# Grouped conv by unshifted blocks, its outer part shifted by DMA

## The chip, the cores and the metric

One core of a Trainium2 chip. The metric is the device time in microseconds (us) of one execution; three executions of the kernel before are shown. The profile is of one further execution.

## The reference

The input x has 128 batches of 64 channels and 1024 positions, in float32. Two layers follow each other, each with a residual:

```python
x = x + _L0_ffn_ref(_L0_cond_ref(x, cond_128, ...), ...)
x = x + _L1_ffn_ref(_L1_cond_ref(x, cond_128, ...), ...)
```

- Layer 0, condition: a 64x64 matrix per batch (a softmax mixture of 8) times the channels, plus a bias per channel.
- Layer 0, ffn: a base product 1024x1024 plus a mixture of 8 low-rank experts of rank 16, gated by a softmax over 8 logits minus a threshold.
- Layer 1, condition: a 1D convolution over the 1024 positions with 9 taps, padding 4, in 4 groups of 16 channels, plus a context value per channel.
- Layer 1, ffn: a base product 1024x1024 plus the same kind of low-rank experts, the two largest of 8 logits weighted by a softmax.

```python
out = lax.conv_general_dilated(x, weight, window_strides=(1,), padding=[(4, 4)],
                               dimension_numbers=('NCH', 'OIH', 'NCH'), feature_group_count=4)
```

## The kernel before, in words

A tile is 128 rows (2 batches x 64 channels) of 1024 positions. There are 64 tiles per layer (STEPS = 64), so 128 steps, n = 0 to 127; layer 1 begins at n = 64. Each float32 operand of a product is split into a high part (float32r) and a low part, and a product is hi x hi + hi x lo + lo x hi.

A step n does on TensorE (`step`, L856) the base product of tile n, and woven into it the condition of tile n+1 (`mix`, L762) and the tail of tile n-1 (`turn`, L814, and `up`, L822):

- `base` (L792, matmuls at L807): for k = 0 to 7, three products of Y's 128 columns k against the weights, each over three PSUM banks of about 387 columns, 9 matmuls per k. It accumulates in psB, 3 banks per parity of n. At k = 0 and 4 it waits for the halves of Yhi and Ylo (`yhi_half`, `ylo_half`).
- `mix`: 4 chunks c, each of two blocks k = 2c, 2c+1 of 128 positions, into bank c % 2 of psT. Chunk c follows base tile k = MIX_AFTER[c], that is k = 0, 1, 2, 3. In layer 0 a block has two matmuls with the mixing matrix M (L781, L782). In layer 1 it has four: for each of two windows w of the input, one of 256 columns (Xhi against CT hi and lo, L787) and one of 128 (Xlo against CT hi, L789).
- `turn` (after k = 4, L820) transposes the gated expert values hw; `up` (after k = 5, L833) adds the expert product to psB with 6 matmuls of 512 columns.

In layer 1 the partition of Xraw is (r, i): r one of 8 residues of the position block, i one of 16 channels of a group, and the free axis is (b, q), b one of 8 blocks of 16 channels (2 batches x 4 groups), q one of 128 position blocks of 8 positions. `load_x` (L209) fetches it from x1_scratch by 8 DMAs, one per r (L222), with a shift of 4 residues, so that 9 taps around a block of 8 outputs lie in the windows q and q+1 of one shifted row; that is why Xraw, Xhi and Xlo have 129 columns per b (QP, XW), one of them zero.

VectorE (DVE), `step` at L714: the gates of tile n-1 (`weigh`, L693, from the copy L699 to hw at L705); `evacuate_y` (L546), two adds per chunk from psT to Y (L566, L568); `split_y` (L570), Ylo by halves (L575); `low_ht` (L709); `add_rest` (L585); `emit` (L592), which writes outb of tile n-1 in three adds (L605) and counts `o_done`.

ScalarE (ACT), `step` at L469: exponentials of the gates, Yhi by halves (L431), Xhi of tile n+2 (`high_x`, L407, L417), the copy HThi of the turned values (`high_ht`, L515). At the last step of layer 0 also the split of layer 1's weights (`split_w`, L443).

GpSimd (POOL), `step` at L367: Xlo of tile n+2 (`low_x`, L327, L333) and the residual plus bias of tile n+1 in res (`residual`, L344, L352 and L362).

SyncE (SP), `step` at L256, issues the DMAs, one queue in this order: Xraw and row of tile n+2 (L213 or L222, L224); the store of tile n-1 (`store`, L297, issue L301) behind a wait for `o_done`; in layer 1 res of tile n+1 (L294). Layer 0 stores into x1_scratch, layer 1 into out.

All orders are written out by hand; the engines meet at counting semaphores. Y is one buffer, Yhi, Ylo, res, outb and Xraw have two, Xhi and Xlo one.

Of the kernel before, what the change touches and what calls it, by code (L numbers as in the profile page):

```python
# [27 lines left out]
P = 128  # L28
# [8 lines left out]
TAPS, PAD = 9, 4  # L37
# [12 lines left out]
QP = Q + 1  # L50
XW = BG * QP
MODES = 8
MIX_AFTER = (0, 1, 2, 3)
MIX_AFTER_FIRST = (1, 3, 4, 5)
TURN_AFTER, UP_AFTER = 4, 5
# [13 lines left out]
def build(nc, x, condw, condr, mixw, l0w, l0b, l0B, convw, l1w, l1b, l1B, out):  # L69
    NT = x.shape[0]  # L70
    STEPS = NT // P
    x1 = nc.dram_tensor("x1_scratch", [NT, H], F32).ap()
    rows = nc.dram_tensor("row_scratch", [2, STEPS, P], F32).ap()
    atts = nc.dram_tensor("att_scratch", [2, STEPS, MODES], F32).ap()

    with ExitStack() as ctx:
# [11 lines left out]
        CT = sb("CT", [P, G, 2, 2, P], F32R)  # L88
        bias = sb("bias", [P, H])

        Xraw = sb("Xraw", [P, 2, XW])
        Xhi, Xlo = sb("Xhi", [P, XW], F32R), sb("Xlo", [P, XW], F32R)
# [6 lines left out]
        mixT = sb("mixT", [P, MODES, C])  # L99
        prod = sb("prod", [P, MODES, C])  # L100
# [62 lines left out]
        pad_zero = sem("pad_zero")  # L163
# [10 lines left out]
        def as_f32(ap):  # L174
            return ap.bitcast(F32)

# [31 lines left out]
        def _(sp):  # L208
            def load_x(j, par, layer):  # L209

                n = 2 * j + par
                if layer == 0:
                    sp.dma_start(Xraw[:, par, 0:H], x[bass.ds(n * P, P), :]).then_inc(x_loaded[par], 16)  # L213
                else:

                    dst = Xraw[:, par, :].rearrange("p (b q) -> p b q", b=BG)
                    m = n - STEPS
                    src = x1[bass.ds(m * P, P), :].rearrange("(b i) (r q) -> r i b q", b=BG, r=BR)
                    for r in range(BR):
# [36 lines left out]
            def step(j, par, lay0, lay, lay1, lay2):  # L256
                n = 2 * j + par
                if lay2 is not None:
# [5 lines left out]
                    if lay2 == 1:  # L264
                        if lay == 0:
                            sp.wait_ge(pad_zero, par + 1)
                        sp.wait_ge(stored[par], 16 * (j - STEPS // 2 + 2))
                    load_x(j + 1, par, lay2)
                if lay == 0 and isinstance(j, int) and n == 0:
# [6 lines left out]
                    for r in range(BR):  # L276
                        to = craw[r * GC:(r + 1) * GC, :, :, :].rearrange("p g w (t o) -> p g w t o", o=GC)

                        sp.dma_start(to[:, :, 0, 0:r + 1, :], convw[:, :, BR - r:BR + 1, :]).then_inc(conv_in, 16)
                        sp.dma_start(to[:, :, 1, r:BR, :], convw[:, :, 0:BR - r, :]).then_inc(conv_in, 16)  # L280
# [15 lines left out]

            def store(j, par, layer):  # L297
# [3 lines left out]
                sp.dma_start(to[bass.ds((n - layer * STEPS) * P, P), :], outb[:, par, :]).then_inc(stored[par], 16)  # L301

            run(sp, step)
            store(STEPS - 1, 1, 1)
            for par in range(2):
                sp.wait_ge(stored[par], 16 * STEPS)
# [3 lines left out]
        def _(pool):  # L310
# [8 lines left out]
            pool.memset(stage[:, :, NW - 1:NW], 0.0).then_inc(consts, 1)  # L319

# [6 lines left out]
            def low_x(j, par, layer):  # L327
                n = 2 * j + par
                w = (H if layer == 0 else XW) // PIECES
# [37 lines left out]
            def step(j, par, lay0, lay, lay1, lay2):  # L367
# [7 lines left out]
                if isinstance(j, int) and n in (STEPS - 2, STEPS - 1):  # L375

                    pool.wait_ge(x_hi, n + 1)
                    pool.wait_ge(x_lo, n + 1)
                    pool.wait_ge(res_ready, n + 1)
                    v = Xraw[:, par, :].rearrange("p (b q) -> p b q", b=BG)  # L380
                    pool.memset(v[:, :, 0:QP:Q], 0.0).then_inc(pad_zero, 1)
# [9 lines left out]
                if isinstance(j, int) and n == 1:  # L391
# [3 lines left out]
                    pool.tensor_tensor(CT[:, :, :, 1, :], craw, as_f32(CT[:, :, :, 0, :]), ALU.subtract)\  # L395
# [6 lines left out]
        def _(act):  # L402
# [4 lines left out]
            def high_x(j, par, layer):  # L407
                n = 2 * j + par
                if layer == 0:
                    act.wait_ge(x_loaded[par], 16 * (j + 1))  # L410
                    w = H
                else:
                    act.wait_ge(g_loaded[par], 16 * BR * (j - STEPS // 2 + 1))
# [506 lines left out]
```

## Time and profile before

| what | value |
|---|---|
| runs | 2238.45, 2239.20, 2239.59 us; median 2239.2 |
| profiled execution | 2237.36 us |
| its span in the trace | 2235.6 us |
| instructions | 40989 |
| TensorE matmuls | 13196, busy 2193.0 us (98%) |
| VectorE, ScalarE, GpSimd busy | 1394.9, 401.7, 858.6 us |
| mean granted TensorE clock | 0.997 |

The profile counts an engine as busy from the start of an instruction to its modelled end; pipelined matmuls overlap. The chain of waits is followed back from the last instruction; "idle before" with an arrow names what ended it. PEld is the weight load of TensorE, which runs beside its matmuls. An x after a group is its count.

### The profile page before, as it was taken

The numbers are of one execution on the slowest core, as the hardware profiler recorded it, in microseconds if no ns is written. First come the engines' busy times: TensorE is split into PE (matmuls) and PEld (weight loads), VectorE is DVE, ScalarE is ACT, GpSimd is POOL, SyncE is SP. The second block draws the span as 40 slices with busy tenths as digits, with TensorE's granted clock in tenths as the row PEclk, the third lists the DMA queues.
The fourth block names the chain that finished last, engine by engine and source line by source line (L and its number), as shares of the span: only waits on it lengthen the run. The fifth ranks groups of instructions, "written<-read, shape, count | busy, mean of one in ns | idle before, by whom it ended". The sixth has DMA issues, their size and how long they took to land.

```text
span 2235.6 us, 40989 instructions
## 1 busy us (share of the span) xinstructions
PE 2193.0 (98%) x13196; PEld 2142.6 (96%) x13196; DVE 1394.9 (62%) x3667; ACT 401.7 (18%) x923; POOL 858.6 (38%) x1053
## 2 busy tenths in 40 slices
PE   4999999999999999999999999999999999999998
PEld 4999999999999999999999999999999999999998
DVE  6777777777777777776655555555555555555554
ACT  3221212121222222222211111111111111111110
POOL 5544444434343434344433333333333333333332
PEclk9999999999999999999999999999999999999999
DMA  5312121111112111213433333334433333333432
GB/s 168 117 60 79 61 73 66 70 70 69 70 69 70 69 70 64 75 60 111 105 93 89 88 88 88 88 88 99 98 94 90 88 88 88 88 88 96 97 95 62
DMA packets 134114, 189.48 MB, mean 85 GB/s; under 512 B 16080, under 2 KB 98384, under 8 KB 134096
## 3 DMA queue, kind: packets, MB, share of 16 engines
q1 hardware_dynamic: 133792, 188.69, 30.3%
q10 hardware_dynamic: 304, 0.56, 0.1%
q8 instruction: 10, 0.16, 0.0%
q14 instruction: 8, 0.07, 0.0%
HBM read 122.01 MB, written 67.18 MB: 85 GB/s over the span
## 4 chain that ended last, share of the span: by engine, by line
PE 96%; DVE 2%; DMA 1%; ACT 1%; issue 0%; POOL 0%; DVEq 0%; SPq 0%; ACTq 0%
PE psB L807 73%; PE psB L833 8%; PE psT L787 7%; PE psT L781 3%; PE psT L789 3%; PE psT L782 1%; PE psB L820 1%; POOL Wlo L324 0%; DVE small L666 0%; DMA outb<-in_condw 0%; DVE prod L526 0%; DMA attb<-att_scratch 0%; ACT Whi L443 0%; DMA Xraw<-in_x 0%; DVE Ylo L575 0%
## 5 line engine op out<-in xcount | busy, mean ns | idle before, releaser
L807 PE MATMUL psB<-Whi,Yhi 128*128 128x384 f32 (+2 forms) x3072 | 748.6, 352 | 3.6 <-issue 3.6
L333 POOL TENSOR_TENSOR Xlo<-Xraw,Xhi 128x256 fp32r<-128x256 f32 (+1 forms) x512 | 423.6, 859 | 785.0 <-ACT Xhi L417 785.0
L807 PE MATMUL psB<-Whi,Ylo 128*128 128x384 f32 (+2 forms) x3072 | 712.3, 340 | 0.0
L807 PE MATMUL psB<-Wlo,Yhi 128*128 128x384 f32 (+2 forms) x3072 | 708.6, 339 | 0.0
L807 PEld LDWEIGHTS psB<-Whi,Ylo 128*128 128x128 f32 x3072 | 558.3, 189 | 0.0
L807 PEld LDWEIGHTS psB<-Wlo,Yhi 128*128 128x128 f32 x3072 | 557.0, 189 | 0.0
L807 PEld LDWEIGHTS psB<-Whi,Yhi 128*128 128x128 f32 x3072 | 517.5, 190 | 19.5 <-issue 3.7
L566 DVE TENSOR_TENSOR Y<-psT,row 128x256 f32<-128x256 f32 x512 | 216.6, 423 | 338.3 <-PE psT L789 318.4
L362 POOL TENSOR_TENSOR res<-res,bias 128x256 f32<-128x256 f32 x256 | 181.5, 742 | 435.5 <-DMA res<-x_scratch 435.5
L431 ACT CAST Yhi<-Y 128x512 fp32r<-128x512 f32 x256 | 159.3, 622 | 897.3 <-DVE Y L568 897.3
L605 DVE TENSOR_TENSOR outb<-psB,res 128x384 f32<-128x384 f32 (+1 forms) x384 | 227.6, 678 | 72.2 <-PE psB L833 65.4
L352 POOL TENSOR_TENSOR res<-Xraw,bias 128x256 f32<-128x256 f32 x256 | 222.8, 903 | 113.9 <-DVE outb L605 113.9
L787 PE MATMUL psT<-CT,Xhi 128*128 128x256 f32 x1024 | 249.0, 320 | 2.6 <-DVE Y L568 1.5
L575 DVE TENSOR_TENSOR Ylo<-Y,Yhi 128x512 fp32r<-128x512 f32 x256 | 212.6, 831 | 46.6 <-ACT Yhi L431 46.6
L789 PE MATMUL psT<-CT,Xlo 128*128 128x128 f32 x1024 | 229.0, 224 | 0.0
L568 DVE TENSOR_TENSOR Y<-psT,Y 128x256 f32<-128x256 f32 x512 | 217.4, 425 | 17.6
L787 PEld LDWEIGHTS psT<-CT,Xhi 128*128 128x128 f32 x1024 | 193.6, 189 | 3.2 <-DVE Y L568 1.8
L789 PEld LDWEIGHTS psT<-CT,Xlo 128*128 128x128 f32 x1024 | 195.3, 191 | 0.0
L417 ACT CAST Xhi<-Xraw 128x1024 fp32r<-128x1024 f32 (+1 forms) x128 | 134.4, 1050 | 163.9 <-PE psT L782 153.8
L781 PE MATMUL psT<-M,Xhi 128*128 128x256 f32 x512 | 132.8, 311 | 21.5 <-DVE M L538 14.9
L699 DVE COPY ag<-psB 128x138 f32<-128x138 f32 (+1 forms) x128 | 38.6, 301 | 167.5 <-PE psB L807 167.5
L781 PEld LDWEIGHTS psT<-M,Xhi 128*128 128x128 f32 x512 | 98.3, 192 | 23.3 <-issue 16.2
(85 smaller groups left out, 1397.7 us busy)
## 6 DMA issues: line engine op xcount, KB each, us to landing
Xraw<-in_x SPq DMA_DIRECT2D x64, 512.0 KB, 3.3
x_scratch<-outb SPq DMA_DIRECT2D x64, 512.0 KB, 2.6
Xraw<-x_scratch SPq DMA_DIRECT2D x512, 64.0 KB, 3.5
res<-x_scratch SPq DMA_DIRECT2D x64, 512.0 KB, 4.7
out<-outb SPq DMA_DIRECT2D x64, 512.0 KB, 3.0
row<-row_scratch SPq DMA_DIRECT2D x128, 64.0 KB, 3.1
stage<-in_l0w SPq DMA_DIRECT2D x8, 580.5 KB, 8.5
stage<-in_l1w SPq DMA_DIRECT2D x8, 580.0 KB, 6.2
```

The source lines that it names most:

```text
L333: last = pool.tensor_tensor(Xlo[:, piece], Xraw[:, par, piece], as_f32(Xhi[:, piece]), ALU.subtract)
L352: last = pool.tensor_tensor(res[:, par, :].rearrange("p (r q) -> p r q", r=BR)[:, r, :], Xraw[:, par, 0:H].rearrange("p (q r) -> p r q", r ...
L362: last = pool.tensor_tensor(res[:, par, piece], res[:, par, piece], bias[:, piece], ALU.add)
L566: nc.vector.tensor_tensor(y, parts[0], add, ALU.add).then_inc(y_part, 1)
L568: nc.vector.tensor_tensor(y, parts[1], y, ALU.add).then_inc(y_chunk, 1)
L575: nc.vector.tensor_tensor(Ylo[:, par, h * HB:(h + 1) * HB], Y[:, h * HB:(h + 1) * HB], as_f32(Yhi[:, par, h * HB:(h + 1) * HB]), ALU.subtr ...
L605: last = nc.vector.tensor_tensor(to[:, r0:r1, :], product, res[:, par, :].rearrange("p (r q) -> p r q", r=BR)[:, r0:r1, :], ALU.add)
L781: mm(to, Xhi[:, xs], M[:, :, :].rearrange("p s n -> p (s n)"), start=True, stop=False)
L787: mm(to, Xhi[:, xs], CT[:, g, w, :, :].rearrange("p s n -> p (s n)"), start=(w == 0), stop=False)
L789: last = mm(to[:, 0:P], Xlo[:, xs], CT[:, g, w, 0, :], start=False, stop=(w == 1))
L807: last = mm(psB[:, 3 * par + b, 0:cols], y, w[:, k, BANK0[b]:BANK0[b] + cols], start=(k == 0 and y is yh and w is Whi), stop=(k == KT - 1 ...
L833: last = mm(psB[:, 3 * par + b, :], y[:, :], w[:, layer, b * HB:(b + 1) * HB], start=False, stop=(y is HTlo), skip_group_check=True)
```

## The change

In layer 1 the input block is no longer shifted. With the 8 positions of a block as residues r, the taps that stay inside the block (the inner part) and those that reach into the block before or behind (the outer part) are two sets of 128 output columns. CT is laid out [group, hi or lo, part, 128]. A block has 3 matmuls of 256 columns: Xhi against CT hi, Xhi against CT lo, Xlo against CT hi, each for both parts at once. VectorE adds the inner part to the row value in Y with one add per chunk; ScalarE copies the outer part to `side` (`copy_side`), and frees the bank by it. Per half of the channels SP issues four DMAs from `side` to `shifted`, one partition down for the first 4 residues and one up for the last 4, each cut in rows 0 to 111 and 112 to 126; VectorE adds `shifted` to Y (`add_shifted`), and only then Yhi and Ylo are made, by halves of the channels.

The chunks of layer 1 are put in pairs behind k = 0 and 1; in steps of layer 1 turn and up are behind k = 2 and 3. `side` shares its memory with mixT and prod of layer 0. Layer 0 stores each tile a second time, in block order, into x1_block_scratch with 8 DMAs of 16 partitions, and layer 1 loads Xraw with one DMA of 512 KB. ScalarE's HThi and Xhi go ahead of the split of Y, VectorE's emit ahead of it.

```diff
-TAPS, PAD = 9, 4
+TAPS, REACH = 9, 4
...
-QP = Q + 1
-XW = BG * QP
+HALF_B = BG // 2
+SHIFT_ROWS = ((0, 112), (112, P - 1))
+SHIFTS = 2 * 16 * len(SHIFT_ROWS)
+STORE0 = 16 * (1 + BG)
 MODES = 8
 MIX_AFTER = (0, 1, 2, 3)
+CONV_AFTER = (0, 0, 1, 1)
 MIX_AFTER_FIRST = (1, 3, 4, 5)
-TURN_AFTER, UP_AFTER = 4, 5
+TURN_AFTER, UP_AFTER = (4, 2), (5, 3)
...
+        shifted = sb("shifted", [P, 2, BR, HALF_B * GC])
...
-                    dst = Xraw[:, par, :].rearrange("p (b q) -> p b q", b=BG)
-                    m = n - STEPS
-                    src = x1[bass.ds(m * P, P), :].rearrange("(b i) (r q) -> r i b q", b=BG, r=BR)
-                    for r in range(BR):
-
-                        first = 1 if r < PAD else 0
-                        sp.dma_start(dst[r * GC:(r + 1) * GC, :, first:first + Q], src[(r + PAD) % BR])\
-                            .then_inc(g_loaded[par], 16)
+                    sp.dma_start(Xraw[:, par, :], x1b[bass.ds((n - STEPS) * P, P), :]).then_inc(g_loaded[par], 16)
...
+                if lay1 == 1:
+                    for h in range(2):
+                        shift(*after(j, par), h)
                 if lay0 is not None:
                     store(*before(j, par), lay0)
...
+            def shift(j, par, h):
+
+                m = 2 * j + par - STEPS
+                sp.wait_ge(side_out, NC * m + 2 * h + 2)
+                if isinstance(m, int) and m == 0:
+                    sp.wait_ge(side_zero, 1)
+                else:
+                    sp.wait_ge(y_sum, 2 * m + h - 1)
+                for p0, p1 in SHIFT_ROWS:
+                    sp.dma_start(shifted[p0 + 1:p1 + 1, h, 0:REACH, :], side[p0:p1, h, 0:REACH, :])\
+                        .then_inc(side_in[h], 16)
+                    sp.dma_start(shifted[p0:p1, h, REACH:BR, :], side[p0 + 1:p1 + 1, h, REACH:BR, :])\
+                        .then_inc(side_in[h], 16)
...
+                if layer == 0:
+                    blocks = x1b[bass.ds(n * P, P), :].rearrange("(r i) (b q) -> b i r q", r=BR, b=BG)
+                    for b in range(BG):
+                        sp.dma_start(blocks[b], outb[b * GC:(b + 1) * GC, par, :].rearrange("p (r q) -> p r q", r=BR))\
+                            .then_inc(stored[par], 16)
...
+            pool.memset(shifted[:, :, :, :], 0.0).then_inc(side_zero, 1)
...
+            def copy_side(j, par, c):
+
+                m = 2 * j + par - STEPS
+                act.wait_ge(y_chunk, NC * (m + STEPS) + c + 1)
...
+                bank = psT[:, c % 2, :].rearrange("p (b s t o) -> p b s t o", b=2, s=2, t=BR)
+                to = side[:, c // 2, :, :].rearrange("p t (b o) -> p b t o", b=HALF_B)
+                b = 2 * (c % 2)
+                nc.scalar.copy(to[:, b:b + 2], bank[:, :, 1]).then_inc(side_out, 1)
...
+                if lay1 == 1:
+                    for c in range(NC):
+                        copy_side(*after(j, par), c)
+                        if last_of_0 and c == 1:
+                            split_w(0, 1)
                 if last_of_0:
-                    for k in range(KT // 2):
+                    for k in range(1, KT // 2):
                         split_w(k, 1)
+                if lay1 == 1 and not last_of_0:
+                    high_ht(*before(j, par))
+                    if lay2 is not None:
+                        high_x(j + 1, par, lay2)
                 if lay1 is not None:
                     split_y(*after(j, par), lay1, range(0, 1))
...
                         y = Y[:, :].rearrange("p (t b o) -> p b t o", t=BR, b=BG)[:, 2 * c:2 * c + 2]
                         add = bcast(row[:, par, c * 2 * GC:(c + 1) * 2 * GC].rearrange("p (b o) -> p b o", b=2), 2, BR)
-                        parts = tuple(bank[:, :, s, :].rearrange("p b (t o) -> p b t o", t=BR) for s in range(2))
-                    nc.vector.tensor_tensor(y, parts[0], add, ALU.add).then_inc(y_part, 1)
-                    dve.wait_ge(y_part, NC * n + c + 1)
-                    nc.vector.tensor_tensor(y, parts[1], y, ALU.add).then_inc(y_chunk, 1)
+                        nc.vector.tensor_tensor(y, bank[:, :, 0], add, ALU.add).then_inc(y_chunk, 1)
+
+            def add_shifted(j, par, h):
+
+                m = 2 * j + par - STEPS
+                dve.wait_ge(side_in[h], SHIFTS * (m + 1))
+                dve.wait_ge(y_chunk, NC * (m + STEPS) + 2 * h + 2)
+                y = y_half(Y[:, :], 1, h)
+                nc.vector.tensor_tensor(y, shifted[:, h, :, :], y, ALU.add).then_inc(y_sum, 1)
...
+                elif lay1 == 1:
+                    evacuate_y(*after(j, par), 1, range(NC))
+                    low_ht(*before(j, par))
+                    add_rest(*before(j, par))
+                    add_shifted(*after(j, par), 0)
+                    emit(*before(j, par), lay0)
+                    split_y(*after(j, par), 1, range(0, 1))
+                    add_shifted(*after(j, par), 1)
+                    split_y(*after(j, par), 1, range(1, 2))
...
+                if layer == 1 and not (isinstance(j, int) and n == STEPS and c < 2):
+                    pe.wait_ge(side_out, NC * (n - STEPS) + c - 1)
+                elif not (isinstance(n, int) and n == 0 and c < 2):
                     pe.wait_ge(y_chunk, NC * n + c - 1)
...
-                        g = k % G
-                        for w in range(2):
-                            xs = slice(k * QP + w, k * QP + w + Q)
-                            mm(to, Xhi[:, xs], CT[:, g, w, :, :].rearrange("p s n -> p (s n)"),
-                               start=(w == 0), stop=False)
-                            last = mm(to[:, 0:P], Xlo[:, xs], CT[:, g, w, 0, :], start=False, stop=(w == 1))
+                        hi, lo = (CT[:, k % G, s, :, :].rearrange("p w n -> p (w n)") for s in range(2))
+                        mm(to, Xhi[:, xs], hi, start=True, stop=False)
+                        mm(to, Xhi[:, xs], lo, start=False, stop=False)
+                        last = mm(to, Xlo[:, xs], hi, start=False, stop=True)
...
+                if layer == 1 and k == 0:
+                    pe.wait_ge(yhi_half, 2 * n + 2)
...
+                    if layer == 1 and k == 0 and y is yl:
+                        pe.wait_ge(ylo_half, 2 * n + 2)
```

## Rows read from the trace of the kernel before

**Rows 1.** The page, busy time and the granted clock in 40 slices.
```profile
PE 2193.0 (98%) x13196; PEld 2142.6 (96%) x13196; DVE 1394.9 (62%) x3667; ACT 401.7 (18%) x923; POOL 858.6 (38%) x1053
...
PEclk9999999999999999999999999999999999999999
```

**Rows 2.** Chain of waits in a step of layer 1: start us, us, what.
```profile
1600.49 0.12 PE psT L787
...
1600.66 0.17 PE psT L787
1600.83 0.06 PE psT L789
...
1610.55 0.11 PE psB L820
...
1612.25 1.46 PE psB L833 x6
1613.71 4.77 PE psB L807 x27
1618.47 0.12 PE psT L787
```

**Rows 3.** Timeline of weight loads in a chunk, first and last of seven starts.
```profile
1600.44 0.19 PEld L787 LDWEIGHTS psT<-CT,Xhi 128*128 128x128 f32 x1
...
1601.14 0.19 PEld L807 LDWEIGHTS psB<-Whi,Yhi 128*128 128x128 f32 x1
```

**Rows 4.** Timeline of the other engines in layer 1, in order of time.
```profile
1600.15 3.50 SPq L222 DMA_DIRECT2D Xraw<-x_scratch  x7
...
1601.49 0.42 DVE L566 TENSOR_TENSOR Y<-psT,row 128x256 f32<-128x256 f32 x1 [0.30 <-PE psT L789]
...
1603.89 2.82 POOL L362 TENSOR_TENSOR res<-res,bias 128x256 f32<-128x256 f32 x4 [7.02 <-DMA res<-x_scratch]
...
1610.39 1.05 ACT L417 CAST Xhi<-Xraw 128x1032 fp32r<-128x1032 f32 x1
...
1610.52 0.69 DVE L575 TENSOR_TENSOR Ylo<-Y,Yhi 128x512 fp32r<-128x512 f32 x1 [0.69 <-ACT Yhi L431]
...
1611.35 0.26 ACT L515 CAST HThi<-psB 128x128 fp32r<-128x128 f32 x1
...
1611.50 0.62 ACT L431 CAST Yhi<-Y 128x512 fp32r<-128x512 f32 x1
...
1613.84 2.23 DVE L605 TENSOR_TENSOR outb<-psB,res 128x384 f32<-128x384 f32 x3 [0.98 <-PE psB L833]
...
1616.93 0.30 DVE L699 COPY ag<-psB 128x136 f32<-128x136 f32 x1 [0.86 <-PE psB L807]
...
1618.96 0.29 DVE L705 TENSOR_TENSOR hw<-ag,small 128x128 f32<-128x128 f32 x1
```

**Rows 5.** The page, DMA issues: count, KB each, median us to landing.
```profile
Xraw<-in_x SPq DMA_DIRECT2D x64, 512.0 KB, 3.3
...
Xraw<-x_scratch SPq DMA_DIRECT2D x512, 64.0 KB, 3.5
res<-x_scratch SPq DMA_DIRECT2D x64, 512.0 KB, 4.7
...
stage<-in_l0w SPq DMA_DIRECT2D x8, 580.5 KB, 8.5
```

**Rows 6.** Timelines of SP and ACT in a step of layer 0.
```profile
603.24 0.35 SPq L301 DMA_DIRECT2D x_scratch<-outb  x1
606.95 0.33 SPq L213 DMA_DIRECT2D Xraw<-in_x  x1
...
612.93 1.05 ACT L417 CAST Xhi<-Xraw 128x1024 fp32r<-128x1024 f32 x1 [2.59 <-PE psT L782]
```

**Rows 7.** Timelines of PE and DVE at the turn of the layers.
```profile
1069.25 0.71 PE L833 MATMUL psB<-Bhi,HThi 128*128 128x512 f32 x2 [0.70 <-DVE HTlo L712]
...
1076.93 2.40 DVE L666 SCALAR_TENSOR_TENSOR small<-small 128x1 f32<-128x1 f32 x1
```

More of the change, by code:

```diff
@@ L98, in build @@
         attb = sb("attb", [P, STEPS, MODES])
-        mixT = sb("mixT", [P, MODES, C])
-        prod = sb("prod", [P, MODES, C])
+        mixbuf = sb("mixbuf", [P, 2, MODES * C])
+        mixT, prod = (mixbuf[:, i, :].rearrange("p (k o) -> p k o", k=MODES) for i in range(2))
+        side = mixbuf[:, :, :].rearrange("p h (t n) -> p h t n", t=BR)
         agg = sb("agg", [P, C])
@@ L162, in build @@
         stored = [sem(f"stored{p}") for p in range(2)]
-        pad_zero = sem("pad_zero")
+        side_zero, side_out, side_in, y_sum = sem("side_zero"), sem("side_out"), [sem(f"side_in{h}") for h in range(2)], sem("y_sum")
         x_hi, x_lo = sem("x_hi"), sem("x_lo")
@@ L328, in low_x @@
                 n = 2 * j + par
-                w = (H if layer == 0 else XW) // PIECES
+                w = H // PIECES
                 pool.wait_ge(x_hi, n + 1)
@@ L572, in split_y @@
                 for h in halves:
-                    dve.wait_ge(y_chunk, NC * n + (2 * h + 2 if layer == 0 else NC))
                     dve.wait_ge(yhi_half, 2 * n + h + 1)
-                    nc.vector.tensor_tensor(Ylo[:, par, h * HB:(h + 1) * HB], Y[:, h * HB:(h + 1) * HB],
-                                            as_f32(Yhi[:, par, h * HB:(h + 1) * HB]), ALU.subtract)\
-                        .then_inc(ylo_half, 1)
+                    nc.vector.tensor_tensor(y_half(Ylo[:, par, :], layer, h), y_half(Y[:, :], layer, h),
+                                            as_f32(y_half(Yhi[:, par, :], layer, h)), ALU.subtract).then_inc(ylo_half, 1)
             def split_w(k, layer):
@@ new lines, in step @@
+                    emit(*before(j, par), lay0)
+                elif lay1 == 1:
+                    evacuate_y(*after(j, par), 1, range(NC))
+                    low_ht(*before(j, par))
+                    add_rest(*before(j, par))
+                    add_shifted(*after(j, par), 0)
+                    emit(*before(j, par), lay0)
+                    split_y(*after(j, par), 1, range(0, 1))
+                    add_shifted(*after(j, par), 1)
+                    split_y(*after(j, par), 1, range(1, 2))
+                else:
+                    low_ht(*before(j, par))
+                    add_rest(*before(j, par))
@@ L856, in step @@
             def step(j, par, lay0, lay, lay1, lay2):
-                mix_after = MIX_AFTER_FIRST if isinstance(j, int) and j == 0 and par == 0 else MIX_AFTER
+                first = isinstance(j, int) and j == 0 and par == 0
+                mix_after = MIX_AFTER_FIRST if first else CONV_AFTER if lay1 == 1 else MIX_AFTER
                 for k in range(KT):
                     base(j, par, lay, k)
-                    if k == TURN_AFTER and lay0 is not None:
+                    if k == TURN_AFTER[lay] and lay0 is not None:
                         turn(*before(j, par))
-                    if k in mix_after and lay1 is not None:
-                        mix(*after(j, par), lay1, mix_after.index(k))
-                    if k == UP_AFTER and lay0 is not None:
+                    for c in range(NC):
+                        if k == mix_after[c] and lay1 is not None:
+                            mix(*after(j, par), lay1, c)
+                    if k == UP_AFTER[lay] and lay0 is not None:
                         up(*before(j, par), lay0)
```

115 lines of the change are left out of this document (58 added, 57 removed).

## Prediction

> **What bounds the kernel now.** I read the page first: TensorE (PE) is busy for 2193.0 of 2235.6 us and its clock is granted in full, 2.4 GHz, in practically every slice [rows 1]. So only what shortens PE's own stream, or makes it wait, moves the time. The chain of waits inside one step of layer 1 then gives PE's order with the start of each piece [rows 2]. One step runs from the conv's first matmul at 1600.49 to the same matmul at 1618.47, 17.98 us, with no wait in it. It holds 8 tiles k of the base product (72 matmuls of on average 387 columns), 4 conv chunks of 8 matmuls, a turn and an up. Three k in a row take 4.77 us [rows 2], so a k is 1.59 and a matmul of 387 columns 0.1767 us; the up is 1.46 and the turn 0.11. What is left for the conv is 17.98 - 12.72 - 1.57 = 3.69 us, 0.92 a chunk, 0.115 a matmul.
>
> That 0.115 is the point. A chunk alternates 256 and 128 columns, on average 192, which at 2.4 GHz is 0.080 us of array time. But the weight loads follow each other at an even pace in it: from 1600.44 to 1601.14 there are six gaps, 0.117 each, whatever the width of the matmul [rows 3]. A matmul of 387 columns (0.161 us of columns) hides its load; one of 128 (0.053) doesn't. The conv pays for its 32 loads, not for its 6144 columns.
>
> **The change, part by part.**
>
> *Conv matmuls.* Per block it has 3 matmuls of 256 columns in place of 2 of 256 and 2 of 128: the columns stay 768, the loads go from 4 to 3. Per step 24 matmuls stand for 32. The price of one of 256 columns after another isn't in the trace. From below it is the load pace as the whole step gives it, 0.115. From above: the 387-column one costs 0.1767 - 0.161 = 0.016 more than its columns; on 0.107 this gives 0.123, and if it came on top of the load pace, 0.131. The nearest row is the first conv matmul of a chunk, 256 columns with its load already hidden behind a base matmul: the next matmul starts 0.12 us later [rows 2]. I take 0.12. Conv per step: 24 x 0.12 = 2.88 us against 3.69, a gain of 0.81. There are 64 such convs (tiles 64 to 127, issued in steps 63 to 126): 64 x 0.81 = 52 us. The ends: 0.115 gives 0.93 and 60 us; 0.131 gives 0.55 and 35 us.
>
> The Trainium skill, "TensorE: Matmul & The Clock Gate", section "Back-to-back issue gap", prices 256 columns at 262 cycles, 0.109 us; its section on LDWEIGHTS gives columns / 1.2, 0.107 us for 128. By an estimate from the page a conv would be 24 x 0.109 = 2.62 us, the gain 68 us and the time 2173. The trace disagrees with it at both neighbours (0.1767 where 387 columns would be 0.164, and 0.117 for the load), so it is rival F and not the sum.
>
> *New order, turn and up at k=2, 3.* Nothing is added on PE. I set the first matmul of a step to 0; base_done of the last step reaches DVE at about +0.05. The tail of the old step's gates ends with hw at 1619.25, +2.4 (step start 1618.47 - 1.59 = 1616.88) [rows 4]. PE: k=0 to 1.6, chunks 0 and 1 to 2.3 and 3.05, k=1 to 4.65, chunks 2 and 3 to 5.4 and 6.1, k=2 to 7.7, turn, k=3 to 9.4, up to 10.85.
>
> *Banks of psT.* They are now freed by ScalarE's (ACT) copy of the outer half. DVE keeps one add of 0.42 per chunk in place of two [rows 4]. ACT's copy of 128x256 isn't in the trace: between the 0.26 of 128 and the 0.62 of 512 columns [rows 4], 0.38. Chunk 0 is evacuated from 2.5 to 2.9 and copied at 3.35, chunk 1 from 3.2 to 3.6 and copied at 4.0. PE wants them at 4.65 and 5.4: slack 1.3 and 1.4. Chunks 2 and 3 are evacuated by 6.65 and copied by 7.1. The turn's copy follows at 7.8 to 8.1, HTlo is there at 8.5, up wants it at 9.4: slack 0.9. Cost 0; without that cover each us of delay is a us of PE.
>
> *Shift.* SP issues 4 DMAs per half (0.35 to 0.5 each; seven took 3.50 [rows 4]). SP is free by then: its load of Xraw, its row and its res go out behind the store of the step before, which moves from o_done at 1616.07 (+17.2) to about +13.1. Half 0: from 4.1 to 6.1. Half 1: from 7.2 to 9.2. An SBUF to SBUF transfer isn't in the trace; small ones from HBM land in 3.5 us, the 512 KB ones in 3.3 to 4.7 [rows 5], so half 1 lands at about 12.7. Then DVE, held by emit from 10.9 to 13.1 (2.23 [rows 4]), splits half 0 to 13.8 and adds half 1 to 14.5 (0.7 each, as the Ylo row), ACT casts it to 15.15, DVE splits it to 15.9. PE wants yhi at 17.15 and ylo 1.06 later. Slack 2.0, and for the landing alone 2.9. Cost 0; the next thing to be late would be this chain. DVE's sum falls by 4 x 0.42 and rises by 2 x 0.7.
>
> The Trainium skill, "DMA: Bandwidth & Descriptors", section "Why a DMA increments its semaphore by 16 and not by 1", says a DMA uses as many engines as the largest divisor up to 16 of its slowest dimension allows, so 127 rows would go to one engine; here 112 and 15 rows get 16 and 15. No row here shows it, and it prices nothing in the sum.
>
> *Other moves.* high_x (1.05) goes ahead of the split of Y, so Xlo is ready earlier. res now lands at +1.3 of the next step and POOL's residual (2.82 [rows 4]) falls beside the gates and the first evacuations. POOL can hold DVE up: a DVE operation on a single column took 2.40 at the turn of the layers, where POOL subtracts 1160 columns at once [rows 7], against 0.30 for the copy of 136 columns [rows 4]. The pieces here are 0.7, so I allow up to 1 us of delay; the slack of 1.3 covers it. Cost 0, with 0.3 per step as the upper end (19 us).
>
> *Layer 0.* A store becomes 9 DMAs, of 0.5 each on SP: from 603.24 to about 607.8 instead of 603.59. The load of x behind it goes out at 607.8 instead of 606.95, lands about 611.5 and is wanted at 612.93 [rows 6]. Cost 0; if the block writes of 512 B slowed the load by over 1.4 us, ACT's casts would follow. The upper end is 0.2 us x 60 = 12.
>
> *Start and turn of layers.* The memset of shifted, 1024 columns, stands at POOL's start, ahead of its first subtract, which waits for an input to be loaded and cast: 0, at most 1 us, once. In step 63, ACT's chain of split_w, copies and casts gets 4 copies longer (1.5 us) while PE arrives at the up about 0.8 earlier; the wait there is 0.70 today [rows 7]. I add 1.5 us, once; ends -1 and 5.
>
> **Sum.** The profiled execution took 2237.4 us (span 2235.6), 1.8 under the median of 2239.2. 2237.4 - 52 + 1.5 = 2187; on the median's scale 2189.
>
> **Rivals.**
> A. *256 after 256 costs more*, 0.131: a hand-over added to each load. For it: the 387-column matmul has such an excess. Against: pairs of 256 and 128 show none. 2239.2 - 35 + 1.5 = 2206.
> B. *Partial stalls*: PE waits 0.2 to 0.5 us in each step for a psT bank or for HTlo, because POOL's residual now lies on DVE's gates. 13 to 32 us back: 2202 to 2221. Against: the slack above.
> C. *The shift of half 1 lands too late*, on the other side. Place: yhi at k=0. It costs nothing up to a landing at +15.6, eats the gain at 16.4, and from there each us is 64 us. The largest landings in the trace, 8.5 us under a full queue [rows 5], would give 17.7: a stall of 2.1 - 0.81 per step, 2239 + 83 = 2322. Against: nothing else is queued at that time.
> D. *The recorded starts are the truth*: in the conv a matmul of 256 is followed after 0.17 and one of 128 after 0.06 [rows 2]. Then 24 x 0.17 = 4.08, 0.39 more per step, 2264. Against: the even loads, and the first of each chunk with 0.12.
> E. *It doesn't get what it is for*: moving turn and up frees nothing, as PE didn't wait there; true, but the gain above doesn't hang on it.
> F. *The load is no floor*: 256 columns cost their columns, 0.107. 24 x 0.107 = 2.57, a gain of 1.12, 72 us, 2169. Against: the even load pace of 0.117 [rows 3]. The Trainium skill's page on TensorE, above, says much the same.
>
> **How the numbers follow.** My forecast 0.77, A 0.08, B 0.05, C 0.04, D 0.03, F 0.01, a stall that just eats the gain 0.02. Forecast's own span 2180 to 2196. The range goes down to 2177 (60 us and the turn of layers 1 us better) and up to 2208, which takes in A and the near part of B. A change of over 0.2% (4.5 us) can be told from none. Faster: forecast, A, B and F, 0.91, rounded down to 0.90; same 0.02; slower C, D and the odd 0.01, 0.08.
>
> **What would show it.** Right: a layer-1 step of about 17.2 us in the chain of waits, 1.44 for a pair of chunks (12 matmuls), PE without idle between steps, the last Ylo of a step about 1 us before PE's step start, a layer-0 step as long as now. Wrong: a pair of chunks of 1.57 (A) or 2.0 (D); idle on PE ahead of psT or L833 released by ACT (B); idle at k=0 released by ACT's Yhi after a DMA (C); a longer step in layer 0.

## The result, and the profile after

The changed kernel takes 2216.9 us (median of 4 runs, 2213.3 to 2217.8) against 2238.8 for the kernel before (4 runs). The ratio is 0.990 with a 95% interval of 0.9883 to 0.9917: 22 us faster, where 50 were forecast, and outside the range of 2177 to 2208. The profiled execution took 2217.8 us, its span is 2216.0.

First the page of the changed kernel: busy time, then the groups of the conv, of the copy that frees its banks and of the add that is left on VectorE (busy us, mean ns, idle before).

```profile
PE 2156.4 (97%) x12684; PEld 2097.3 (95%) x12684; DVE 1440.5 (65%) x3539; ACT 503.3 (23%) x1179; POOL 847.9 (38%) x1052
...
L614 DVE TENSOR_TENSOR Y<-psT,row 128x256 f32<-128x256 f32 x256 | 102.1, 417 | 100.9 <-PE psT L853 100.7
L470 ACT COPY mixbuf<-psT 128x256 f32<-128x256 f32 x256 | 89.6, 374 | 324.3 <-DVE Y L614 324.3
L851 PE MATMUL psT<-CT,Xhi 128*128 128x256 f32 x512 | 150.4, 294 | 13.1 <-ACT mixbuf L470 12.3
```

There are 512 matmuls fewer, as meant, and TensorE is still the bound, but it now waits. The waits of TensorE in the changed kernel (total us, times, longest us) name two places: the banks of psT, freed by ScalarE's copy into side (the tile mixbuf), where the kernel before had a single wait of 1.5 us for VectorE, and HTlo ahead of up, where it had 1.5 us in two waits.

```profile
PE psT L851 <- ACT mixbuf L470: 12.3, 31, 2.6
PE psB L901 <- DVE HTlo L764: 7.9, 3, 6.3
```

This list is too short for the first place. It counts idle time from the modelled end of a matmul, 0.28 us after its start, although the next one can start after 0.12, so a delay of up to 0.16 doesn't appear in it. The lengths of the steps, below, show all of it.

The chain of waits shows what a layer-1 step is when nothing holds it, against [rows 2]:

```profile
1615.05 0.12 PE psT L851
1615.16 0.12 PE psT L852
...
1616.48 1.60 PE psB L875 x9
...
1619.52 1.59 PE psB L875 x9
1621.10 0.11 PE psB L888
...
1622.83 1.40 PE psB L901 x6
1624.23 7.95 PE psB L875 x45
1632.18 0.12 PE psT L851
```

Twelve matmuls of 256 columns take 1616.48 - 1615.05 = 1.43 us, 0.119 each, and the step 1632.18 - 1615.05 = 17.13. The starts of L888 (the turn) give every step's length. From these, before and after:

| | before | after | difference |
|---|---|---|---|
| 62 steps of layer 1 | 17.99 each | 17.47 each (17.11 to 17.82) | -32 us; -53 if each were 17.14 |
| turn of step 63 to turn of step 64 | 21.97 | 27.97 | see below |
| steps of layer 0, mean | 16.087 (16.05 and 16.12 in turns) | 16.127 (all alike) | +2.5 us |

The turn of the layers has to be read with care, since turn itself moved from k=4 to k=2: undisturbed the interval would have been 17.98 before and 17.14 - 2 x 1.59 = 13.96 after. It was 4.0 over before and 14.0 over after, so it costs 10 us more. The account is: conv -54.6 (64 x 0.853), stalls in layer 1 +20.8 (62 x 0.336), turn of the layers +10.0, layer 0 +2.5, sum -21.3, against -19.6 between the two spans. The other 1.7 us lie ahead of the third turn, at 99.6 us before and 101.3 after. That start varies from profile to profile (101.2 in e9_pad, which is the kernel before with one unused tile, 101.0 to 103.0 in the variants of the change), so it isn't assigned to the change.

**Stalls in layer 1.** VectorE, TensorE and GpSimd in one held step, timeline of the changed kernel:

```profile
1595.82 0.30 DVE L751 COPY ag<-psB 128x136 f32<-128x136 f32 x1 [1.56 <-PE psB L875]
...
1596.85 0.16 DVE L737 RECIPROCAL small<-small 128x1 f32<-128x1 f32 x1
1596.93 0.68 DVE L738 TENSOR_SCALAR small<-iota,small 128x8 f32<-128x8 f32 x1
1597.64 0.66 DVE L740 SCALAR_TENSOR_TENSOR small<-iota,small 128x8 f32<-128x8 f32 x1
1598.33 0.67 DVE L743 TENSOR_SCALAR small<-small 128x8 f32<-128x8 f32 x1
1599.03 0.78 DVE L757 TENSOR_TENSOR hw<-ag,small 128x128 f32<-128x128 f32 x1
1599.74 0.74 DVE L614 TENSOR_TENSOR Y<-psT,row 128x256 f32<-128x256 f32 x2
```
```profile
1600.69 0.39 PE L851 MATMUL psT<-CT,Xhi 128*128 128x256 f32 x1 [0.28 <-ACT mixbuf L470]
```
```profile
1596.85 2.82 POOL L395 TENSOR_TENSOR res<-res,bias 128x256 f32<-128x256 f32 x4 [5.93 <-DMA res<-x_scratch]
```

GpSimd starts its residual at 1596.85, in the middle of the gates. From then on each of four gate operations lasts about as long as one of the residual's pieces (2.82 / 4 = 0.7). The gates end at 1599.81, 3.99 us after the start of the copy of ag, where it was 2.32 before (1616.93 to 1619.25 in [rows 4]). The RECIPROCAL that started together with the residual kept its 0.16.

The 62 steps of this one trace say the same. The longer the gates, the longer the step:

| gates, copy of ag to hw, us | steps | length of the step, us |
|---|---|---|
| under 3.4 | 10 | 17.11 to 17.14 |
| 3.4 to 3.6 | 9 | 17.19 to 17.25 |
| 3.6 to 3.8 | 12 | 17.29 to 17.41 |
| 3.8 to 4.0 | 9 | 17.45 to 17.67 |
| over 4.0 | 22 | 17.68 to 17.82 |

So the slack was about 1.1 us over the undisturbed 2.25, near the 1.3 of the prediction, and what lies above it goes into the step.

**Turn of the layers.** The chain of waits in the changed kernel, from SP's issue to the up:

```profile
1068.18 7.46 DMA shifted<-mixbuf
...
1075.66 0.70 DVE Y L622
...
1076.45 0.63 ACT Yhi L457
...
1077.71 0.29 DVE HTlo L764
...
1078.14 2.90 PE psB L901 x6
```

The four copies of this half land 7.5 to 8.6 us after their issue; the medians of all are 2.3 us (112 rows) and 2.0 (15 rows). SP's timeline says what was ahead of it in the queue: four weight tiles of 580 KB, a tile of Xraw and the bias, 3.3 MB within 4 us.

```profile
1062.14 2.08 SPq L304 DMA_DIRECT2D stage<-in_l1w  x4
1064.39 0.38 SPq L229 DMA_DIRECT2D Xraw<-x_block_scratch  x1
1064.81 0.47 SPq L230 DMA_DIRECT2D row<-row_scratch  x1
1065.32 0.44 SPq L293 DMA_DIRECT2D bias<-in_l1b  x1
1065.87 0.62 SPq L319 DMA_DIRECT2D shifted<-mixbuf  x1
```

A second wait of 2.6 us follows in step 64, ahead of the third chunk (L851). There one operation of the gates lasts 2.67 us beside GpSimd's subtract of 1160 columns. Timelines of VectorE and GpSimd:

```profile
1087.36 2.67 DVE L712 TENSOR_SCALAR small<-small 128x8 f32<-128x8 f32 x1
```
```profile
1087.32 2.69 POOL L357 TENSOR_TENSOR Wlo<-stage,Whi 128x1160 fp32r<-128x1160 f32 x1
```

The clock of TensorE fell too. The up took 2.90 us there and not 1.40, and the next matmuls of the base product were as slow. From 1076.2 to 1083.0 us, beginning inside the wait of 6.3 us, and again from 1093.3 to 1096.7, beginning at the end of the wait of 2.6, 1.2 GHz were granted in place of 2.4. The kernel before had 2.4 GHz through its whole turn of the layers, with waits of 0.7, 1.1 and 1.5 us. The first stretch: its length, busy us of PE, PEld, DVE, ACT and POOL, and behind them the granted share of the clock, 0.50:

```profile
1076.20:1083.00 6.80, 4.86 (x13) 4.32 (x14) 5.01 (x10) 4.47 (x6) 1.23 (x1) 0.50 0.00 0
```

So the 10 us more have two parts. The waits of TensorE between the two turns add up to 9.6 us (6.3, 0.7, 2.6) against 3.3 before, 6.3 more. The clock makes about 4, an estimate: half of the 4.9 and 3.3 us for which TensorE was busy in the two stretches.

### The profile page after: what moved, and what is told of

It reads as the page before. It is cut to its first block, busy times and chain, and to the rows that moved or that the text cites. A ratio compares the mean times of both kernels' runs of the same rounds, so it can differ in the third digit from the quotient of the medians.

```text
span 2216.0 us, 41456 instructions
## 1 busy us (share of the span) xinstructions
PE 2156.4 (97%) x12684; PEld 2097.3 (95%) x12684; DVE 1440.5 (65%) x3539; ACT 503.3 (23%) x1179; POOL 847.9 (38%) x1052
## 4 chain that ended last, share of the span: by engine, by line
PE 88%; DVE 6%; issue 2%; DMA 1%; ACT 1%; SPq 1%; POOL 0%; DVEq 0%; ACTq 0%
PE psB L875 68%; PE psB L901 8%; PE psT L847 3%; PE psT L851 3%; PE psT L853 2%; PE psT L852 2%; PE psT L848 1%; DVE small L738 1%; DVE small L743 1%; DVE small L740 1%; PE psB L888 1%; DVE Y L614 1%; ACT mixbuf L470 1%; DMA Xraw<-in_x 0%; SPq L332 0%
## 5 line engine op out<-in xcount | busy, mean ns | idle before, releaser
L875 PE MATMUL psB<-Whi,Yhi 128*128 128x384 f32 (+2 forms) x3072 | 737.1, 348 | 5.6 <-issue 5.6
L366 POOL TENSOR_TENSOR Xlo<-Xraw,Xhi 128x256 fp32r<-128x256 f32 x512 | 410.3, 833 | 796.9 <-ACT Xhi L441 796.9
L875 PEld LDWEIGHTS psB<-Whi,Yhi 128*128 128x128 f32 x3072 | 526.8, 190 | 22.4 <-issue 5.8
L441 ACT CAST Xhi<-Xraw 128x1024 fp32r<-128x1024 f32 x128 | 134.7, 1052 | 165.3 <-PE psT L848 152.0
L614 DVE TENSOR_TENSOR Y<-psT,row 128x256 f32<-128x256 f32 x256 | 102.1, 417 | 100.9 <-PE psT L853 100.7
L470 ACT COPY mixbuf<-psT 128x256 f32<-128x256 f32 x256 | 89.6, 374 | 324.3 <-DVE Y L614 324.3
L851 PE MATMUL psT<-CT,Xhi 128*128 128x256 f32 x512 | 150.4, 294 | 13.1 <-ACT mixbuf L470 12.3
L764 DVE TENSOR_TENSOR HTlo<-psB,HThi 128x128 fp32r<-128x128 f32 x128 | 37.3, 292 | 173.5 <-ACT HThi L562 173.5
L852 PE MATMUL psT<-CT,Xhi 128*128 128x256 f32 x512 | 145.1, 283 | 0.0
L853 PE MATMUL psT<-CT,Xlo 128*128 128x256 f32 x512 | 145.1, 283 | 0.0
L851 PEld LDWEIGHTS psT<-CT,Xhi 128*128 128x128 f32 x512 | 97.8, 191 | 28.4 <-ACT mixbuf L470 26.7
```

What stands on the lines that cost most here:

```text
L366: last = pool.tensor_tensor(Xlo[:, piece], Xraw[:, par, piece], as_f32(Xhi[:, piece]), ALU.subtract)
L851: mm(to, Xhi[:, xs], hi, start=True, stop=False)
L852: mm(to, Xhi[:, xs], lo, start=False, stop=False)
L853: last = mm(to, Xlo[:, xs], hi, start=False, stop=True)
L875: last = mm(psB[:, 3 * par + b, 0:cols], y, w[:, k, BANK0[b]:BANK0[b] + cols], start=(k == 0 and y is yh and w is Whi), stop=(k == KT - 1 ...
```

## The experiments

The theories are **T**, the residual beside the gates causes the stalls of layer 1; **Q**, the queue and the order of work cause the turn's; **M**, the new place of turn and up is what gives the shift its room; **A**, the 0.04 us of layer 0 come from where the operands lie. Comparisons are with the kernel before, run beside each.

### e1_gates: residual behind the gates

```diff
                         pool.wait_ge(bias_in, 32)
+                    pool.wait_ge(hw_ready, n)
                     pool.wait_ge(r_loaded[par], 16 * (j - STEPS // 2 + 1))
```

> Edit: in layer 1 GpSimd's residual of tile n waits until VectorE's gates of tile n-1 are done (hw_ready), so that it no longer runs beside them. Theory T (the residual, which now starts 1 us into a step, holds four gate operations up by 0.4 us each, so the copies that free the psT banks come late and TensorE waits 0.35 us a step): every step of layer 1 is 17.13 us, idle before L851 outside the turn of the layers is 0, about 20 us less than the change as it stands: 2197. Rival R (the pairs of chunks leave no room for the bank's two readers in any case): the waits before L851 stay, 2215 or more. Rival S (the residual only moves onto the adds of the evacuation and slows those instead): half of the gain or less, 2207 to 2217.

Measured 2196.9 us, ratio 0.981 (0.9797 to 0.9827). All 62 steps of layer 1 are 17.13 or 17.14 us. VectorE's timeline, and GpSimd's, which now begins at hw:

```profile
1606.41 0.30 DVE L752 COPY ag<-psB 128x136 f32<-128x136 f32 x1 [1.55 <-PE psB L876]
...
1607.53 0.27 DVE L739 TENSOR_SCALAR small<-iota,small 128x8 f32<-128x8 f32 x1
1607.84 0.23 DVE L741 SCALAR_TENSOR_TENSOR small<-iota,small 128x8 f32<-128x8 f32 x1
1608.10 0.23 DVE L744 TENSOR_SCALAR small<-small 128x8 f32<-128x8 f32 x1
1608.45 0.29 DVE L758 TENSOR_TENSOR hw<-ag,small 128x128 f32<-128x128 f32 x1
1608.82 0.42 DVE L615 TENSOR_TENSOR Y<-psT,row 128x256 f32<-128x256 f32 x1
```
```profile
1608.91 2.82 POOL L396 TENSOR_TENSOR res<-res,bias 128x256 f32<-128x256 f32 x4 [7.66 <-DVE hw L758]
```

T holds: one wait on GpSimd takes 20 us off. Rival S falls too. The adds of the evacuation (L615, one operand in PSUM, one in SBUF) take 0.42 us beside the residual, as they did without it: half of the 248 adds of layer 1 ran beside it, with the same mean. Of the operations in the rows above, those that were held have two inputs in SBUF or a scalar from SBUF. The Trainium skill, "SBUF — State Buffer", section "SBUF: two separate sides", says this of the port pair that VectorE and GpSimd share: it goes to one of them for a whole instruction, and only VectorE instructions with two SBUF inputs or in a two-port mode want it. The rows agree for hw, which has two inputs in SBUF (0.29 to 0.78), and for the add from PSUM (0.42 unchanged); that the held operations of 8 columns (0.27 to 0.68) ran in a two-port mode isn't shown by any row.

### e2_spread: more slack instead

```diff
-CONV_AFTER = (0, 0, 1, 1)
+CONV_AFTER = (0, 0, 2, 2)
-TURN_AFTER, UP_AFTER = (4, 2), (5, 3)
+TURN_AFTER, UP_AFTER = (4, 3), (5, 4)
```

> Edit: the second pair of chunks follows k=2 instead of k=1, turn and up follow k=3 and 4 in layer 1; the residual still runs beside the gates. Theory T (the gates end up to 1.7 us late, and the first bank's slack of 1.3 us isn't enough): with 1.6 us more of slack the waits before L851 are gone although the gates are as slow as before, steps of 17.13, time 2197 to 2200. Rival C (the shift chain has no room): TensorE waits for Yhi at k=0 instead, each step 17.3 or more.

Measured 2194.9 us, ratio 0.9805 (0.979 to 0.982), 2 us under the expected range, steps of 17.14 us, no wait before L851 outside the turn of the layers. But the expectation had "the gates are as slow as before", and that was wrong. Groups of VectorE between 1200 and 2100 us, in the changed kernel and in e2 (count, busy us, mean ns):

```profile
L757 DVE TENSOR_TENSOR hw<-ag,small 128x128 f32<-128x128 f32 x51 | 37.5, 735 | 4.0
L738 DVE TENSOR_SCALAR small<-iota,small 128x8 f32<-128x8 f32 x51 | 25.3, 496 | 0.0
```
```profile
L757 DVE TENSOR_TENSOR hw<-ag,small 128x128 f32<-128x128 f32 x52 | 15.2, 293 | 4.1
L738 DVE TENSOR_SCALAR small<-iota,small 128x8 f32<-128x8 f32 x52 | 14.2, 273 | 0.0
```

With up 1.6 us later, emit, the store and the load of res are later too, and the residual came past the gates without being asked to: it starts 2.4 to 3.9 us after the copy of ag, where the gates take 2.25; in the changed kernel it is 0.7 to 1.9 in nearly every step. So e2 cures the stall by the cause of e1, and whether slack alone would do it wasn't tried. It also shows that the shift chain has room for a second half issued 1.6 us later.

### e4_queue: nothing large ahead of the first shift

In step 62 the four weight loads go ahead of the store, in step 63 the bias behind the shift:

```diff
-                if isinstance(j, int) and n == STEPS - 1:
-
-                    sp.dma_start(bias[:, :], l1b.partition_broadcast(P)).then_inc(bias_in, 16)
+                if isinstance(j, int) and n == STEPS - 2:
+                    load_w1(range(KT // 2, KT))
                 if lay1 == 1:
                     for h in range(2):
                         shift(*after(j, par), h)
+                if isinstance(j, int) and n == STEPS - 1:
+                    sp.dma_start(bias[:, :], l1b.partition_broadcast(P)).then_inc(bias_in, 16)
...
```

> Edit: the loads of the last four weight tiles of layer 1 are issued ahead of the store in step 62, and the bias of layer 1 behind the shift in step 63, so that the first shift doesn't queue behind them. Theory Q (2.8 MB ahead of it in the queue make the first shift land about 7 us late; that makes the wait of 6.3 us before L901 and takes the clock down): the wait before L901 falls to under 2.5 us, the step of the turn from 27.97 to about 22, time 2211. Rival (the wait comes from the order on ScalarE and VectorE, where four weight casts stand ahead): the wait stays over 4 us, 2215 or more.

Measured 2209.3 us, ratio 0.987 (0.9853 to 0.9884). The interval from turn to turn fell from 27.97 to 24.73, not to 22, and the wait before L901 from 6.3 to 5.0, not to under 2.5: Q holds for the transfer, whose copies land in 2.0 to 3.0 us now, and only in part for the wait. VectorE's timeline says why:

```profile
1070.73 2.92 DVE L638 TENSOR_TENSOR Wlo<-stage,Whi 128x1160 fp32r<-128x1160 f32 x1 [2.56 <-ACT Whi L485]
1073.57 3.11 DVE L626 TENSOR_TENSOR Y<-shifted,Y 128x512 f32<-128x512 f32 x1
```

The transfer now is there in time, and the add that takes it, 0.7 us elsewhere, takes 3.11 beside GpSimd's subtract of 1160 columns. Of the 7.6 us against the change as it stands only 3.2 are the turn's; most of the rest is in the stalls of layer 1, which differ from profile to profile (over 17.14: 20.8 us in the change, 13.9 here, and 14.5 to 22.4 in e3, e6 and e9_last, which don't touch them). That the time came near the expected 2211 is luck.

The turn's interval varies as well. In e9_last, which changes only where a tile lies, it is 26.0 us, in e6 28.0, in e5 28.1. What differs is the clock: e9_last has one stretch at 1.2 GHz, of 6.9 us, the other two have a second one of 3.4 us. So a difference of under 2 us in this interval shows nothing by itself. Here there is one stretch of 3.5 us, against 10.2 us in the changed kernel, so a part of the 3.2 us is the clock's.

### e3_ht: HTlo ahead of the split of Y in step 63

```diff
-                if lay1 == 1 and not last_of_0:
+                if lay1 == 1:
                     high_ht(*before(j, par))
...
+                    low_ht(*before(j, par))
+                    add_rest(*before(j, par))
                     add_shifted(*after(j, par), 0)
                     split_y(*after(j, par), 1, range(0, 1))
-                    low_ht(*before(j, par))
-                    add_rest(*before(j, par))
```

> Edit: in step 63 HThi and HTlo are made before the split of Y, not behind it. Theory Q2 (the wait before L901 is there because HTlo stands behind the add of the shifted half, which waits for the transfer): the wait of 6.3 us before L901 goes to about 2 us, set by the weight casts, though Y then comes late at k=0 of step 64 and takes part of it back; the turn of the layers 27.97 to 24 or 25, time 2213. Rival (weight casts and subtracts set the wait by themselves): it stays over 5 us and the time 2217.

Measured 2215.6 us, ratio 0.989 (0.9878 to 0.9908); turn to turn 24.97, the wait before L901 0.5 at the turn. As expected, a good part comes back at k=0 of step 64, a wait of 5.9 us. With 5 us of spread between the runs the time alone would not tell this from the change; the intervals of the trace do.

### e7_all and e8_pieces: together, and GpSimd's subtracts cut

e7 is e1, e4 and e3 in one. e8 adds:

```diff
-                pool.tensor_tensor(Wlo[:, k, 0:w], stage[:, k, 0:w], as_f32(Whi[:, k, 0:w]), ALU.subtract)\
-                    .then_inc(w_loP, 1)
+                cut = 1 if layer == 0 else 4
+                for i in range(cut):
+                    piece = slice(i * w // cut, (i + 1) * w // cut)
+                    last = pool.tensor_tensor(Wlo[:, k, piece], stage[:, k, piece], as_f32(Whi[:, k, piece]),
+                                              ALU.subtract)
+                last.then_inc(w_loP, 1)
```

> Edit: e1 and e4 together, and HThi and HTlo ahead of the split of Y in step 63. If the causes add up: steps of 17.13 (20 us), the turn of the layers 27.97 to about 21 (7 us), time 2190. If the subtracts on GpSimd hold VectorE at the turn in any case: the turn of the layers stays at 24 or more, time 2194.

> Edit: e7, and in layer 1 GpSimd subtracts each weight tile in four pieces of 290 columns instead of one of 1160. If a GpSimd subtract holds VectorE until it is over: the VectorE operations of 2.4 to 3.1 us at the turn shrink to under 1.1, the turn of the layers gets 1 to 3 us shorter than in e7. Rival (VectorE is slowed by the whole of GpSimd's work and not by the length of one operation): no difference to e7.

e7: 2193.4 us, ratio 0.980 (0.9784 to 0.981), turn to turn 23.60, nearer to the 24 of the rival, in which GpSimd's subtracts hold VectorE, than to the 21 of a full sum. e8: 2191.1 us, ratio 0.979 (0.9773 to 0.980), turn to turn 22.19. Of the subtracts, timeline of e8:

```profile
1069.64 1.80 DVE L643 TENSOR_TENSOR Wlo<-stage,Whi 128x1160 fp32r<-128x1160 f32 x1 [2.56 <-ACT Whi L490]
...
1071.89 0.77 DVE L631 TENSOR_TENSOR Y<-shifted,Y 128x512 f32<-128x512 f32 x1
```

The operations that lasted 2.92 and 3.11 in e4, and 2.92 and 2.64 in e7, last 1.80 and 0.77: here a VectorE operation lost at most the length of the one GpSimd operation in its way. More operations meet a piece, though: four that follow took 1.25 to 1.97, where the same ones in e7 took 0.68 to 1.35. The intervals of e7 and e8 overlap, so as times they are one. The turn's interval doesn't part them either: e8's is 1.4 us shorter, but its waits add up to 5.8 us and e7's to 5.7, and e8 has 1.2 GHz for 6.9 us and e7 for 10.3. So the cut shortens the held operations; that it shortens the kernel isn't shown. Both beat the kernel before and the changed one.

### e5_narrow: is it the load?

```diff
-                        last = mm(to, Xlo[:, xs], hi, start=False, stop=True)
+                        last = mm(to[:, 0:P], Xlo[:, xs], CT[:, k % G, 0, 0, :], start=False, stop=True)
```

> Edit: the third matmul of a conv block (Xlo by CT hi) takes only the 128 inner columns, which leaves the low part of the input out of the outer taps. Theory L (a conv matmul costs its weight load, 0.117 us, whatever its columns): 12 matmuls take 1.40 us against 1.43 now, nothing else moves. Rival C (256 columns cost their columns, 0.107 plus an excess, 0.12): the four narrow ones save 0.06 each, 12 matmuls take 1.2 us.

Chain of waits of e5, a pair of chunks:

```profile
1613.77 0.12 PE psT L851
1613.89 0.12 PE psT L852
1614.01 0.06 PE psT L853
1614.07 0.17 PE psT L851
...
1615.12 1.65 PE psB L875 x9
```

Measured 2211.6 us, one run. A step that nothing holds is 17.03 where it was 17.13: 8 matmuls lost half of their columns, 0.43 us of array time, and gave 0.10. That is near the 0.06 of theory L and far from the 0.48 of rival C. By the recorded starts the pair takes 1.35 us and not 1.40, but the nine base matmuls behind it then take 1.65 and not 1.60, so the step is the safer measure. Each matmul of these kernels has a weight load of its own, so the runs can't tell the load from any other fixed cost of a matmul. It settles the rival about the recorded starts as well: a start 0.06 behind the matmul of 128 and 0.17 behind the next one of 256 is how the record shows the same even pace.

### e12_late and e11_single: turn and up back at k=4 and 5

Both carry e1's wait.

```diff
-TURN_AFTER, UP_AFTER = (4, 2), (5, 3)
+TURN_AFTER, UP_AFTER = (4, 4), (5, 5)
```

and e11 also has `CONV_AFTER = (0, 1, 2, 3)`.

> Edit: e1 (residual behind the gates), but turn and up of layer 1 stay behind k=4 and 5 as before the change; the pairs of chunks stay. Theory M (the place of turn and up is what gives emit, and behind it on VectorE the second shifted half, their room): up ends at +14.0, emit at +16.2, Yhi of the second half at +18.2 and not at +15.2, so TensorE waits for it at k=0 and a step is 18.0 to 18.4 us, the time 2245 to 2265, no gain over the kernel before. Rival (my rival E as I wrote it: moving turn and up frees nothing): 17.14 as in e1, 2197.

> Edit: as e12, and the chunks one by one behind k=0, 1, 2, 3, so that only the new conv and the shift are left of the change to TensorE's order. The shift of the second half is issued 3 us later and lands about +15.5, still before VectorE comes to it behind emit, so the step is as in e12 or up to 0.5 us longer: 18.0 to 18.8. Rival: 17.14, if the shift has more room than I think.

e12: 2278.9 us, ratio 1.018 (1.0162 to 1.0196), steps of 18.41. e11: one run of 2275.8, steps of 18.41. The waits of TensorE in e12:

```profile
PE psB L876 <- ACT Yhi L458: 64.3, 62, 1.1
```

M holds, with VectorE's order as the change has it. Without this part of it the change, e1's wait included, is 40 us slower than the kernel before. The step of 18.41 is at the upper end that I gave; the time is 14 above my bound of 2265, which didn't follow from that step: 62 x (18.4 - 17.14) on e1's 2197 is 2275. e11 equals e12, so the single chunks cost nothing more. What sets the step is emit on VectorE, not the transfer: the chain of waits of e12 goes from up over emit, Ylo of the first half and the add of the second to Yhi. VectorE was idle for 1.6 us just before emit. The second half's copies are issued by 1613.5 in the same step and land 2 us later, before up begins, so an order with this half ahead of emit might do without the move of turn and up. It wasn't tried.

### e6_nostore, e9_pad, e9_last: layer 0

e6 leaves the store in block order out and loads layer 1's input from the other copy. e9_pad is the kernel before with an unused tile of 4 KB per partition ahead of bias; e9_last is the changed kernel with shifted allocated last.

```diff
+        unused = sb("unused", [P, H])
         bias = sb("bias", [P, H])
```

> Edit: layer 0 stores each tile once, as before the change, and layer 1 loads its input from that row-order copy, so the conv sees rows in the wrong order; this leaves the block-order store out. Theory D (the second store costs the layer-0 step its 0.04 us, 16.13 against 16.085, by memory traffic beside TensorE's reads): the step is 16.085 again and the time 3 us lower than that of the change. Rival (the 0.04 comes from elsewhere, such as where the operands lie): it stays 16.13.

> Edit: the kernel before with one unused tile of 1024 columns where the change puts shifted, so that all tiles behind it lie 4096 bytes further. Theory A (where the operands lie sets the 0.04 us of the layer-0 step): the layer-0 step moves from 16.087 to 16.127 or otherwise off its value. Rival: it stays at 16.087, and time at 2239.

> Edit: the changed kernel with shifted allocated last, behind all other tiles. Theory A: the layer-0 step goes back from 16.127 towards 16.087. Rival: it stays at 16.127.

The layer-0 step is 16.127 in e6 and e9_last and 16.087 in e9_pad (one run each: 2212.0, 2218.1, 2238.4). Neither the second store nor the place of that tile makes the 0.04 us. What does stays open; it is 2.5 us in all. One trait that the mean hides: in the kernel before and in e9_pad every second step is shorter, 16.05 and 16.12 in turns, and in the changed kernel and its variants none is.

## Why the prediction was wrong

**Conv matmuls: right.** The step says "I take 0.12" and 0.81 a step; 0.119 and 0.85 came, 54.6 us against 52. The cause, a cost of each matmul that hardly depends on its columns up to 256, is shown by e5; that it is the weight load fits the even load pace and isn't shown apart. The Trainium skill, "TensorE: Matmul & The Clock Gate", section "Back-to-back issue gap", made 0.109 of it, which is 0.010 too low, as it was 0.013 too low for the 387 columns in the trace of the kernel before; rival F, which it spoke for, is out.

**Other moves: the step that failed.** I saw that the residual would fall beside the gates, cited the row with 2.40, allowed 1 us of delay and let "the slack of 1.3 cover it". The slack was about right (1.1); the delay was wrong. It was 1.67 in the step shown and up to 1.9 in others: four operations, each held for up to one piece of the residual. The rows had what a count needs: a piece is 2.82 / 4 = 0.7 us [rows 4], so four operations can lose up to 2.8, more than the slack. That each lost about 0.4 came only with the trace after. Cost 0 was put, 0.336 a step came (20.8 us); my upper end of 0.3 was about its size. That is rival B, mechanism, place and price, with a chance of 0.05. Its range of 2202 to 2221 held the result, in part by luck: on the forecast of 2189 these stalls alone give 2210, and the turn of the layers makes most of the rest.

**Start and turn of layers: mis-sized.** I added 1.5 us with an upper end of 5; it was 10. I counted ScalarE's work and the wait before the up, not the queue: 3.3 MB issued just ahead of the first shift (e4), the add behind it, which GpSimd holds once the queue is clear (e4, e8), HTlo behind both (e3), the gates of step 64 held for 2.67 us, and the clock that fell in the pauses (about 4 us, an estimate). The bias and weight loads stand in the code I had read; I checked the queue in the steady step alone.

**Shift: right in the steady step.** Issue of four took 2.9 us, not 2.0; landing 2.3 us, not 3.5; they even out. TensorE waits for it in no step behind the turn of the layers. Two numbers of rival C don't stand: the largest landings in the trace before were 12.3 us (the bias of layer 0) and 11.8, not 8.5, and "nothing else is queued at that time" holds for the steady step alone.

**Turn and up at k=2, 3: rival E was wrong as written.** "Moving turn and up frees nothing" holds for the kernel before. In the new one its undoing costs 82 us (e12 against e1), with VectorE's order left as it is. The change was no sum of parts, one part made room for another.

**Layer 0.** The load of x had the room I gave it; the 0.04 us a step are open.

**The sum.** Against the forecast the stalls cost 20.8 us, the turn of the layers 8.5 (10.0 where 1.5 were put) and layer 0 2.5; the conv gave 2.6 more. That is 29.2, for the 28 us between 2189 and 2216.9.

## What to carry to other kernels

At 2.4 GHz a float32r matmul with its own weight load took 0.117 us in a mix of 128 and 256 columns and 0.119 with 256 alone, so fewer, wider matmuls gain at equal columns. When an operation on GpSimd moves in time, list the VectorE operations it will meet, count those with two inputs in SBUF or a scalar from it, and charge each with up to one GpSimd operation's length; a single wait that moves GpSimd off the critical stretch took all of the stalls away here (e1). For a new small transfer look at the queue where it is fullest, not in the steady step.

## What the runs showed of the hardware

- An SBUF to SBUF copy of 112 rows of 1 KB lands 2.3 us after issue, of 15 rows in 2.0; SP needs 0.55 to 0.95 us to issue one, against 0.33 for a load of 512 KB.
- A VectorE operation of 8 columns (L712) with a median of 0.44 us in the changed kernel took 2.67 there beside a GpSimd subtract of 1160 columns, and 0.29 in e8 at the same place.
- 124 adds of a PSUM and an SBUF operand took 0.42 us beside GpSimd's residual, as 124 others did without it (e1).
- At 1.2 GHz the up of six matmuls of 512 columns took 2.90 us, at 2.4 GHz 1.40 (the changed kernel).
